# Early-fusion block on one core: three orders changed in the attention stage (contexts' copy, a third of the second contexts product, token rows' transposes)

## What is computed

```
h = concat(patch_tokens(x), txt)                      # 32 x 165 x 192
h = h + linear_attention(layernorm(h))                # no softmax
z = layernorm(layernorm(h)); q, k, v = z @ in_w.T     # 12 heads of 16
x = u + softmax(q k / 4) v @ out_w.T                  # u: the normed h
x = x + gelu(x @ mlp_w1) @ mlp_w2
x = x + sum over the 2 best of 4 experts
out = h + x
```

## Time and profile before

| | |
|---|---|
| Runs | 1290.51, 1297.41, 1303.87 us |
| Profiled execution | 1291.37 us, its span 1289.6 us |
| Granted TensorE clock, mean over the span | 0.988 |
| Busy: TensorE, VectorE, ScalarE, GpSimd | 93%, 75%, 54%, 32% |
| Chain that ended last: PE, DVE, ACT | 67%, 15%, 5% |

### The profile page before, as it was taken

The page is one execution under the profiler, slowest core; times in us unless marked ns, Lnnn a source line. Parts: engine busy times, 40 slices in busy tenths (PEclk is TensorE's granted clock), DMA queues, the critical chain, the costliest instruction groups (busy, mean ns, idle before and its releaser), DMA issues.

```text
span 1289.6 us, 28371 instructions
## 1 busy us (share of the span) xinstructions
PE 1198.8 (93%) x9874; PEld 1024.6 (79%) x9874; DVE 969.3 (75%) x2677; ACT 693.3 (54%) x1630; POOL 412.9 (32%) x397
## 2 busy tenths in 40 slices
PE   7899999999999999999987899999898999999994
PEld 6677777777777777777775799998787899988994
DVE  4677778778877778777866677777778887888783
ACT  1366555565466555665466754554544556555551
POOL 2101111111101111111100137877756455455444
PEclk8999999999999999999999999999999999999997
DMA  2482022201211012201400434446566666766662
GB/s 106 124 209 62 19 57 56 64 21 50 64 56 56 23 57 56 64 21 51 104 9 10 204 56 85 88 83 177 122 172 168 163 155 178 183 165 159 180 158 29
DMA packets 95388, 124.51 MB, mean 97 GB/s; under 512 B 9383, under 2 KB 87592, under 8 KB 91344
## 3 DMA queue, kind: packets, MB, share of 16 engines
q1 hardware_dynamic: 71743, 102.48, 26.8%
q0 software_dynamic: 23568, 21.06, 10.6%
HBM read 70.68 MB, written 52.83 MB: 96 GB/s over the span
## 4 chain that ended last, share of the span: by engine, by line
PE 67%; DVE 15%; issue 8%; ACT 5%; POOL 3%; DMA 1%; DVEq 0%; POOLq 0%; SPq 0%; ACTq 0%
PE PS L1592 55%; PE PS L1595 12%; DVE K L1174 2%; POOL expert_rows L731 1%; DVE st L1086 1%; DVE rec L1196 1%; DMA consts<-in_attn_const 1%; ACT PT L785 1%; ACT GF L978 1%; DVE CN L1197 1%; DVE ZS L1144 1%; ACT PX L810 1%; ACT XAT L785 1%; DVE CNT L1202 1%; DVE X L1209 1%
## 5 line engine op out<-in xcount | busy, mean ns | idle before, releaser
L1592 PE MATMUL PS<-w2r,GH 128*120 (+1 forms) x828 | 248.0, 363 | 1.3 <-DVE GL L1343 0.5
L658 POOL TENSOR_TENSOR rs<-ve,minus_half 128x3 f32<-128x3 f32 (+1 forms) x80 | 58.7, 734 | 556.7 <-DVE ve L1091 556.7
L769 POOL DMA_INDIRECT out<-YO,ids x94 | 162.7, 1731 | 160.5 <-DVE flag L1544 89.2
L978 ACT ACTIVATE GF<-PS,b1c 128x480 f32<-128x480 f32 (+1 forms) x216 | 138.6, 643 | 134.5 <-PE PS L1592 121.3
L1592 PE MATMUL PS<-w2r,GL 128*120 (+1 forms) x828 | 208.5, 252 | 0.0
L810 ACT ACTIVATE PX<-PS,nb 128x165 f32<-128x165 f32 x576 | 176.6, 416 | 46.9 <-DVE nb L1162 46.6
L1592 PE MATMUL PS<-XH,w1r 128*128 128x480 f32 (+1 forms) x432 | 168.5, 392 | 15.7 <-ACT GF L978 9.2
L1592 PEld LDWEIGHTS PS<-w2r,GH 128*120 128x120 f32 x828 | 150.7, 182 | 4.2 <-DVE GL L1343 2.9
L1592 PEld LDWEIGHTS PS<-w2r,GL 128*120 128x120 f32 x828 | 153.0, 185 | 0.0
L1167 DVE COPY PT<-PS 128x384 f32<-128x384 f32 x144 | 80.2, 557 | 88.1 <-PE PS L1595 84.7
L1595 PE MATMUL PS<-ident,PX 128*128 128x128 f32 x864 | 130.8, 281 | 9.4 <-ACT PT L785 8.3
(11 more groups left out here) (270 smaller groups left out, 2342.9 us busy)
## 6 DMA issues: line engine op xcount, KB each, us to landing
w1r<-expert_w_parts SPq DMA_DIRECT2D x25, 1536.0 KB, 7.5
expert_rows<-empty SPq DMA_DIRECT2D x45, 369.4 KB, 6.0
RT<-expert_rows SPq DMA_DIRECT2D x22, 369.4 KB, 3.8
X<-x_scratch SPq DMA_DIRECT2D x11, 360.0 KB, 4.0
out<-X POOLq DMA_DIRECT2D x11, 360.0 KB, 5.6
XP<-in_patches SPq DMA_DIRECT2D x32, 108.0 KB
H<-in_txt SPq DMA_DIRECT2D x16, 192.0 KB, 3.9
out<-H SPq DMA_DIRECT2D x16, 192.0 KB
```

What stands on the lines that cost most here:

```text
L658: nc.gpsimd.tensor_tensor(rs[:, k - 1, 0:n], ve[:, k - 1, 0:n], eps_half[:, 0:n], ALU.pow).then_inc(rstd_ready[k - 1], 1)
L769: nc.gpsimd.indirect_dma_start(out[:, :], bass.IndirectOffsetOnAxis(ap=ids[:, i, t:t + 1], axis=0), YO[:, i % 2, t, :], None, bounds_check ...
L978: nc.scalar.activation(GF[:, m % 3, 0:n], PS[:, 2 + m % 2, 0:n], ACT.Gelu, bias=bias, scale=1.0).then_inc(gelu_ready, 1)
L1592: return nc.tensor.matmul(o, l, r, start=start, stop=stop)
```

## The change

Three orders are changed. No instruction is added or removed, and no wait's value changes.

1. VectorE: `normedT(i)` (the two copies to CNT) stands ahead of `keys(i + 1, 2)`, no longer behind it.
2. TensorE: part c = 0 of `contexts_T(i, 1)` stands ahead of `patch_tokens(i + 2)`; parts 1 and 2 stay behind it.
3. TensorE: `scores(i, 2)` moves behind `tokens_T(i + 1)`, so the token rows' transposes come directly behind `transpose_probs(i, 0)`.

```diff
@@ VectorE, body
                 contexts(i, 2)
+            if core:
+                normedT(i)
             if lin:
                 keys(i + 1, 2)
-            if core:
-                normedT(i)
-            if lin:
                 keys(i + 1, 1)
@@ TensorE
-        def contexts_T(i, b):
+        def contexts_T(i, b, cs=range(3)):
...
-            for c in range(3):
+            for c in cs:
...
-            last.then_inc(ctxT_ps, 1)
+            if c == 2:
+                last.then_inc(ctxT_ps, 1)
@@ TensorE, body
                 transpose_probs(i, 0)
-                scores(i, 2)
                 if not lin:
                     pe.wait_ge(v_ready, i + 1)
                     keep_running(6, 6)
             if lin:
                 tokens_T(i + 1, core)
             if core:
+                scores(i, 2)
                 transpose_probs(i, 1, 2)
...
                 transpose_probs(i, 16, 17)
-            if not core:
+                contexts_T(i, 1, (0,))
+            else:
                 keep_running(4, 8)
             if patch:
                 patch_tokens(i + 2)
             if core:
-                contexts_T(i, 1)
+                contexts_T(i, 1, (1, 2))
```

More of the change, by code:

```diff
@@ L1278, in body @@
                 contexts(i, 2)
-            if lin:
-                keys(i + 1, 2)
             if core:
@@ L1283, in body @@
             if lin:
+                keys(i + 1, 2)
                 keys(i + 1, 1)
```

## The result

The changed kernel took 1315.80 us (median of 4 runs, 1309.65 to 1320.77); beside it the kernel before took 1296.29 (1290.51 to 1303.87). The ratio is 1.0132, 95% interval 1.0079 to 1.0185: slower by 1.3%, where 1.0% was forecast. (The quotient of the two medians is 1.0151, inside the interval. The profiled execution took 1309.65 us, its span 1307.9 against 1289.6.

The account below looks back on a forecast made before the run. TensorE was taken to set the time, with VectorE critical for 11 us of each pair. Terms of +6.3, -1.1 and +7.7 gave +12.9 us on 1297.4, predicted as 1310 us, range 1299 to 1319.

Parts of the forecast that it names:

- The chain: In each attention pair, VectorE is critical without a break from about 256 us to the end of X at 266.88.
- Part 1: VectorE idles before the CNT copies and X comes later: 0.50 us per pair lost, +6.3 us in sum.
- The 0.70 that `project` was to gain: On TensorE, with the CNT wait gone, `project` could start at about 260.7 in place of 261.41.
- the 0.34 before nb: VectorE's gap at the head of the hardware loop, taken as loop bookkeeping that stays and absorbs nothing.
- the rival that made the gap TensorE's: The wait before nb is TensorE's, so part 1 costs 0.16 in the loop: 1306 us; 12 in 100.
- the 0.2 that was forecast: ScalarE's last Q copy comes 0.2 us late for `values` on TensorE, covered by the grown X wait.
- Part 2: A third of the contexts product fills the XNT gap, but `z_T` waits for ve: 0.08 us per pair gained, -1.1 in sum.
- only the distance from 296.18 to 296.27 can be had: Of the 0.42 us XNT gap, only 0.08 per pair before `z_T` on TensorE can be gained.
- Part 3: Token rows' transposes stall on VX for 0.9 to 1.0 us, replacing a 0.40 wait: +0.55 per pair, +7.7 in sum.
- dragged along: Rival: the later unit 2 delays ScalarE, shifting by 0.9 per pair, not 0.55; 4.9 us more, 1315; 8 in 100.
- Faster by slack on VectorE: Rival: VectorE has slack between contexts and X, all three waits are saved, 21.7 us gained, 1276; 7 in 100.
- UB moving off XA: Rival: GpSimd's UB no longer overlaps VectorE's XA copies, `v_ready` comes 0.55 earlier, 1302.6 us; 3 in 100.

Follow-up runs that it names:

- part 1 alone: Only `normedT(i)` moved ahead of `keys(i + 1, 2)` on VectorE, against the kernel before: 1296.64 us, ratio 1.0047, period 42.04 us.
- part 3 alone: Only `scores(i, 2)` moved behind `tokens_T(i + 1)` on TensorE, against the kernel before: 1297.52 us, ratio 1.0041, period 42.02 us.
- the second comparison: The changed kernel run once more, unaltered, beside fresh runs of the kernel before: median 1317.96 us beside 1300.61, ratio 1.0133.
- the copies on ScalarE: The kernel before with the two CNT copies moved from VectorE to ScalarE, no other change: 1294.07 us, ratio 0.9952, period 41.05 us.
- one or both filled: Changed kernel with unread identity transposes before the X wait, the VX wait or both: profiled 1306.91, 1302.44, and 1304.72 and 1304.79 us.

## Why the prediction was right, and where it was not

*The chain.* "From about 256 us on VectorE without a break" to X is shown: part 1 alone moved X by what it inserted, and work taken off that stretch shortened the period.

*Part 1*, 0.50 a pair: measured 0.50. The 0.70 that `project` was to gain came as 0.73. That the 0.34 before nb is the loop's own is shown too: it stands at all 12 turns of the hardware loop (0.33 to 0.37, before and after the change) and not at the written-out boundaries next to it. There the kernel before has 0.20 at the loop's entry and, at its exit, this:

```profile
638.30 0.17 DVE L1091 TENSOR_SCALAR ve<-mv 128x3 f32<-128x3 f32 x1
638.58 1.19 DVE L1162 TENSOR_REDUCE nb<-PS 128x6 f32<-128x990 f32 x1
```

That is a gap of 0.11; in the changed kernel, with TensorE's scores earlier, the two are 0.03 and 0.01. So the rival that made the gap TensorE's (period 41.7) is out for the loop and was right at its two ends, where part 1 cost 0.33 and 0.40 (the forecast had 0.4 and 0.5). The new Q wait of 0.25 is the 0.2 that was forecast, and it is covered.

*Part 2*, -0.08 a pair: measured 0.00. The step that failed is "only the distance from 296.18 to 296.27 can be had". I let Z's transposes follow ve at 0.05 us, the delay of the CNT wait; they followed at 0.14 before and 0.16 after. Too small to matter, 1.1 us of the sum.

*Part 3*, 0.55 from a range of 0.48 to 0.60: measured 0.48, the end at which TensorE follows VX at once. ScalarE was not dragged along: part 3 alone has no new wait for it, and its period is not 42.4.

*The sum.* The forecast was 12.9. The profiled executions differ by 18.3 us: 12.6 are the undisturbed periods, 0.98 a pair with 0.81 at the entry, 4.6 are the three pairs at the lower clock, 1.5 us each, which no term had, 3.2 lie behind the last XN transposes and -2.1 ahead of the first. The medians differ by 19.5 and, in the second comparison, 17.4, which is 4 to 7 us beyond the forecast. The second trace has three long pairs as well, but how much of the medians' excess they are is not shown, since the other executions have no trace. I had the two standstills, their sizes and their distance in my reckoning, and did not ask what TensorE's clock would do behind them. With three long pairs in the sum, about 17.5 us or 1.4%, the chance for slower by over 1% would have been well above 0.46. That the forecast of 1310 held against 1315.80 is the work of the three terms, two of them about right and the third too small to matter, and of a range that was wide enough for the missing one.

*The rivals.* Faster by slack on VectorE: refuted by part 1 alone. UB moving off XA: not seen, VX came where it was expected, and the median of XA is 646 ns in the changed kernel too. What fell besides is my own estimate for the copies on ScalarE, which overlooked what keys 1 waits for.

## What to carry to other kernels

Before a wait is removed, follow the chain past it: here two of the three waits (CNT, XNT) were really measures of how late another engine was, and the third (XAT, 0.40) could be removed only by asking for VX 0.8 us too soon. Work moved ahead on the other engine, or TensorE made to ask for its result sooner, only moved the standstill and in two cases made it longer. Where the critical engine alternates, take work off the one that the chain runs on in that stretch, or fill its idle time with something whose input is ready; reordering with a new wait in it costs that wait. And count new standstills of TensorE together with their neighbours: two of about 1 us cost an extra 1.5 us in a quarter of the pairs.

## What the runs showed of the hardware

- Two standstills of 1.08 to 1.12 and 0.82 us with 1.6 us of work between them were followed by a fall of the granted clock in 6 of 24 pairs (0.50, the 1.2 GHz level, over 3.4 us in the pair shown); the two pairs at the loop's entry, where the first standstill is 0.68, had none. With one standstill alone there was none in 26 pairs, with one or both filled none in 52. The fill was nothing but transposes of the identity, and the clock stayed at 1.00 behind it.
- At a turn of the hardware loop 0.33 to 0.37 us stand between two VectorE instructions, and an input that is ready 1.5 us ahead does not shorten it; at a written-out boundary the same two are 0.01 to 0.03 apart when the input is ready.
- The XA instructions of VectorE that run beside GpSimd's additions (UB) take 646 ns; the same form on Z, with nothing beside it, takes 375.
